# Graph attention and a quantised linear layer on one core: sums per 32 nodes on four column strips, last stage issued among the gathers

## The reference, cut to what matters

```
h   = layernorm(x);  xp = (h @ W).reshape(N, 4, 256)
e   = leaky_relu(a_src[src] + a_dst[dst])            # edges and one loop per node
ee  = exp(e - max over the edges of dst)
out[dst] = sum(ee * xp[src]) / sum(ee)               # per head
x   = x + relu(out + bias)
x   = x + fp6_blocks(layernorm(x)) @ fp6_blocks(weight).T + ffn_bias
```

## Time and profile before

| | us |
|---|---|
| three runs | 1359.40, 1360.31, 1364.32 |
| median | 1360.31 |
| span of the profiled execution | 1363.2 |
| `normalise` (until its last DVE operation ends) | 0 to 129 |
| `project` (until POOL starts its first gather) | 129 to 466 |
| `aggregate` (until the last sum is added) | 466 to 1052 |
| `finish` | 1052 to 1363 |

### The profile page before, as it was taken

How to read it: one execution, slowest core, us unless ns; L and a number is a source line. 1 busy time by engine, 2 the same in 40 slices (tenths; PEclk the granted TensorE clock), 3 DMA queues, 4 the chain that set the end, 5 groups by cost and what they waited for, 6 DMA issues and landing times. The chain is left out here.

```text
span 1363.2 us, 29337 instructions
## 1 busy us (share of the span) xinstructions
PE 1276.4 (94%) x10053; PEld 895.9 (66%) x10053; DVE 1070.2 (79%) x2221; ACT 988.2 (72%) x2239; POOL 747.8 (55%) x677
## 2 busy tenths in 40 slices
PE   7898888999999789999999899999996799999997
PEld 5776444554445378888888788888886344455543
DVE  6998899889844478888888788888885977777771
ACT  3666888884456388998888899899995566666661
POOL 1000766661247377777777777777772344444441
PEclk9899999999999899999999999999999899999999
DMA  7785586543454689999999999999998577777743
GB/s 260 248 301 191 167 309 193 187 154 133 153 210 171 245 323 381 378 368 361 376 360 380 394 401 375 375 336 369 376 369 314 158 192 190 188 191 189 190 101 53
DMA packets 111554, 361.54 MB, mean 265 GB/s; under 512 B 22108, under 2 KB 22892, under 8 KB 111156
## 3 DMA queue, kind: packets, MB, share of 16 engines
q0 software_dynamic: 68192, 225.42, 47.8%
q1 hardware_dynamic: 39860, 133.38, 28.1%
q10 hardware_dynamic: 3360, 0.91, 0.2%
HBM read 297.76 MB, written 72.82 MB: 272 GB/s over the span
## 5 line engine op out<-in xcount | busy, mean ns | idle before, releaser
L1800 PE MATMUL sum_ps<-xg,wgt 128*128 128x256 f16 x4992 | 561.4, 273 | 18.5 <-DMA xg<-d_xp,tables 10.7
L1771 ACT ACTIVATE wgt<-hot,tables 128x128 f16<-128x128 f16 x1664 | 503.1, 388 | 73.4 <-DVE hot L1715 63.2
L1800 PEld LDWEIGHTS sum_ps<-xg,wgt 128*128 128x128 f16 x4992 | 472.5, 98 | 75.3 <-DMA xg<-d_xp,tables 11.8
L1696 POOL DMA_INDIRECT xg<-d_xp,tables x404 | 418.0, 1035 | 127.5 <-issue 119.0
L1569 PE MATMUL xp_ps<-acc 128*128 128x512 f16 x1152 | 263.1, 381 | 8.2 <-DVE acc L1122 5.6
L1755 DVE TENSOR_TENSOR acc<-sum_ps,acc 128x1024 f32 x220 | 268.9, 1222 | 1.1 <-issue 1.0
L2198 PE MATMUL fmm_ps<-xg,tables 128*128 128x512 f16 x1200 | 263.1, 379 | 1.4 <-DVE tables L2027 1.4
L2198 PEld LDWEIGHTS fmm_ps<-xg,tables 128*128 128x128 f16 x1200 | 117.4, 98 | 137.8 <-issue 1.9
L1569 PEld LDWEIGHTS xp_ps<-acc 128*128 128x128 f16 x1152 | 109.3, 98 | 129.3 <-issue 4.9
L1726 DVE TENSOR_TENSOR wgt<-hot,tables 128x512 f16<-128x512 f16 x416 | 157.6, 418 | 0.0
L1929 POOL TENSOR_TENSOR tables<-tables,finv 128x1024 f32<-128x1024 f32 x24 | 45.9, 1914 | 131.8 <-DVE finv L2015 131.8
(11 more groups left out here) (328 smaller groups left out, 1586.7 us busy)
## 6 DMA issues: line engine op xcount, KB each, us to landing
d_xnT<-acc SPq DMA_DIRECT2D x25, 512.0 KB, 3.6
own_row<-d_own SPq DMA_DIRECT2D x25, 512.0 KB, 5.6
wdT<-in_x_dram SPq DMA_DIRECT2D x24, 512.0 KB, 4.9
acc<-d_xnT SPq DMA_DIRECT2D x24, 512.0 KB, 5.2
d_xp<-acc SPq DMA_DIRECT2D x24, 512.0 KB, 3.0
d_own<-acc SPq DMA_DIRECT2D x24, 512.0 KB, 4.3
xr<-in_x_dram SPq DMA_DIRECT2D x24, 512.0 KB, 6.7
out_dram<-acc SPq DMA_DIRECT2D x24, 512.0 KB, 6.7
```

What stands on the lines that cost most here:

```text
L1696: nc.gpsimd.indirect_dma_start(out=xg[s][u][:, :, :].rearrange("p a n -> p (a n)"), out_offset=None, in_=d_xp, in_offset=bass.IndirectOffs ...
L1771: last = nc.scalar.activation(wgt[k % WB][:, u, h, :], hot[k % TURN][:, u, :], ACT.Copy, scale=col(numT[:, h, :], u, q))
L1800: last = nc.tensor.matmul(sum_ps[s][:, h * C:(h + 1) * C], w[:, u, a * HEADS + h, :], x[u][:, b, h * C:(h + 1) * C], start=(u == 0 and h % ...
```

## The change

The sums are taken per window of 32 nodes. 98 windows cut the 391 groups into 488 slots, each of one group and one window, with one gather each; rows of a group outside the window are left out of the transfer. The four heads of a slot are four products with 32 columns of weights, whose outputs are PSUM partitions 0 to 31, 32 to 63, 64 to 95 and 96 to 127, all in one bank of 258 columns (256 and two for the sums of the weights). So the one-hots are 32 wide, all weights of a slot are 256 columns, and DVE makes both halves of them; ACT makes none. DVE adds 258 columns for each slot, at an index that it reads before each.

```diff
+WIN = 32
+TILE_WINS = P // WIN
+WINS = -(-N // WIN)
+GROUPS = -(-E // P)
+SLOTS_ALL = GROUPS + WINS - 1
+KCOLS = 4 * P
+KT = SLOTS_ALL
+AW = C + 2
+READY = [(r + 1) * SLOTS_ALL // SORTED for r in range(SORTED)] + [SLOTS_ALL]
+TURN_AT, MULTIPLY_AT = 16, 18
+RING = 6
...
+            def slot(k):
+                j, s, p, u = PLACES[k][0], sum_ps[k % SB], k // PAIR, k % PAIR
+                if u == 0:
+                    pe.wait_ge(wgt_ready, p + 1)
+                pe.wait_ge(arrived[j], landed[k])
+                if k >= SB:
+                    pe.wait_ge(added, k - SB + 1)
+                for i, (a, b) in enumerate(((0, 0), (0, 1), (1, 0))):
+                    for h in range(HEADS):
+                        nc.tensor.matmul(s[h * WIN:(h + 1) * WIN, 0:C], wgt[p % WB][:, u, a * HEADS + h, :], xg[j][:, b, h * C:(h + 1) * C],
+                                         start=(i == 0), stop=(i == 2), skip_group_check=True)
+                for h in range(HEADS):
+                    last = nc.tensor.matmul(s[h * WIN:(h + 1) * WIN, C:AW], hot[k // HOTS % HB][:, k % HOTS, :], numT16[:, k, h:V:HEADS, 0],
+                                            start=False, stop=True, skip_group_check=True)
+                last.then_inc(slot_done, 1)
...
+            def add(k):
+
+                w = dve.value_load(tile_row[0:1, k:k + 1], min_val=0, max_val=WINS - 1)
+                dve.wait_ge(slot_done, k + 1)
+                if k >= 1:
+                    dve.wait_ge(added, k)
+                to = sums[:, bass.ds(w, 1), :].rearrange("p o n -> p (o n)")
+                nc.vector.tensor_tensor(out=to, in0=sum_ps[k % SB][:, 0:AW], in1=to, op=ALU.add).then_inc(added, 1)
```

```diff
+    CHUNK = 5
+    MIX_AT, X1_AT, ROOT_AT, SCALE_AT, RESCALE_AT, LOW_AT, FINAL_AT = 1, 9, 11, 13, 15, 18, 30
+    BEGIN = READY[0:LAST] + [READY[LAST] + X1_AT + 1]
...
+            for k in range(SLOTS_ALL):
...
+                add(k)
+                for turns, do in due:
+                    for r in turns.get(k + 1, ()):
+                        do(r)
...
+            for k in range(SLOTS_ALL + MULTIPLY_AT + len(every)):
+                if k < SLOTS_ALL:
+                    slot(k)
+                for r in turns.get(k + 1, ()):
+                    turned(r)
+                for r, first, behind in chunks.get(k + 1, ()):
+                    products(r, first, behind)
```

More of the change, by code:

```diff
@@ L38, with ring_of_slots @@
 EP = EC * P
[L40 to L60, removed]
+WIN = 32
[6 more added lines that the diff above has]
+AW = C + 2
+assert SLOTS_ALL <= KCOLS and SLOTS_ALL % 4 == 0
+SORTED = TILES - 1
+READY = [(r + 1) * SLOTS_ALL // SORTED for r in range(SORTED)] + [SLOTS_ALL]
+TURN_AT, MULTIPLY_AT = 16, 18
+RING = 6
+SPARE_TILES = range(1, 6)
+def ring_of_slots():
+    free_from = [(0, j) for j in range(RING)] + [(READY[j] + TURN_AT + 8, RING + n) for n, j in enumerate(SPARE_TILES)]
+    used, places = {}, []
+    for k in range(SLOTS_ALL):
+        j = min((used.get(b, -1), b) for since, b in free_from if since <= k)[1]
+        places.append((j, used.get(j)))
+        used[j] = k
+    return places
+PLACES = ring_of_slots()
+FRESH = [k for k, (_, before) in enumerate(PLACES) if before is None]
 HCOLS = 17
@@ L242, in program @@
         if upto >= 3:
[L243 to L255, removed]
+            gather_and_finish(nc, maker, locals())
 def normalise(nc, maker, g):
@@ new lines, in _ @@
+            own.link(nc.vector.tensor_reduce(out=order_f[:, 0:SORTED], in_=compared, axis=AX.X, op=ALU.add))
+            nc.vector.tensor_copy(order_i[:, 0:SORTED], order_f[:, 0:SORTED])
+            dve.wait_ge(made, 3)
+            for c in range(CH):
+                last = nc.vector.tensor_scalar(inside[:, c, :], real(upto_f), kcol[:, c:c + 1], None, ALU.is_gt)
+            own.link(last)
+            for c in range(CH):
+                last = nc.vector.scalar_tensor_tensor(out=inside[:, c, :], in0=real(before_f), scalar=kcol[:, c:c + 1],
+                                                      in1=inside[:, c, :], op0=ALU.is_gt, op1=ALU.subtract)
@@ L1093, in _ @@
             for c in range(CH):
[L1094 to L1096 removed]
+                gather(nrow[c], halves(d_num), step_i[:, c:c + 1], rows_in)
             highest(range(5, TILES))
@@ L1610, in _ @@
                     last.then_inc(cinT_done, 1)
-                places = [(c, u, slice(u * P, (u + 1) * P), u * KCOLS + c * P) for c in range(CH) for u in range(SUB)]
                 if t == BUSY + 5:
@@ L1959, in _ @@
+            for k in range(SLOTS_ALL):
+                gather(k)
         @block.vector
@@ new lines, in final @@
+            def final(r):
+                dve.wait_ge(mm_done, OPENED + r + 1)
+                nc.vector.scalar_tensor_tensor(out=xr[r % 3], in0=mm_ps[:, :], scalar=out_scale[:, :], in1=xr[r % 3],
+                                               op0=ALU.mult, op1=ALU.add).then_inc(final_ready, 1)
+            steps = [(FINAL_AT, final), (LOW_AT, low), (RESCALE_AT, rescale), (SCALE_AT, scales), (ROOT_AT, root), (X1_AT, x1), (MIX_AT, mix)]
+            due = [(pieces(at), do) for at, do in steps]
@@ L2225, in _ @@
-            pe.wait_ge(ps_written, bias_set(LAST))
-            pe.wait_ge(low_ready, whole(LAST))
-            for half in range(2):
-                for c in range(KC):
-                    for a, b in ((0, 0), (0, 1), (1, 0)):
-                        last = product(LAST, c, a, b, half, c == KC - 1 and a == 1)
-                last.then_inc(mm_done, 1)
+            spin = numT16.rearrange("p k v b -> p (k v b)")
+            for half in range(2):
+                last = nc.tensor.matmul(mm_ps[:, half * 512:(half + 1) * 512], iota16[:, :], spin[:, 0:512], start=True, stop=True)
```

993 lines of the change are left out of this document (407 added, 586 removed).

## The result

The changed kernel takes 1542.8 us (median of 4 runs, 1541.0 to 1543.6), the one before 1359.9 beside it: a ratio of 1.1335, 95% interval 1.1316 to 1.1353. The forecast was 1495, in a range of 1310 to 1590, with 0.74 for slower. The profiled execution has a span of 1539.2 us, 41 us more than the 1498 of the sum. Among the executions of the last four experiments and of the kernel before beside them, two single ones took over 3300 us in a slow state; the times given leave them out.

What follows compares the result with a forecast made beforehand. PE was taken as full in the gathers and last stage, POOL full too. Start 481, plus 46 to slot 28, 22 tiles by 40.0 = 880, and 91 uncovered gave 1498, so 1495 us by median; range 1310 to 1590.

Steps and rivals of the forecast that it cites:

- End of the first stage: DVE's chain before the gathers: about 60 small operations replace some 30, net +14.5 us; POOL's first gather moves 466 to 481.
- the 46 us before slot 28: From POOL's first gather to the first tile's DVE-bound part: ten gathers, 6.1 us to land, 18 gathers by 1.33 us.
- A slot on PE: PE's products for one slot: 0.43 us if the four strips run beside one another, 1.39 if not.
- Strips one after another: Rival, chance 0.06: strips don't run side by side; 1.39 us a slot on PE, 49.6 us a tile, 1706 in all.
- A slot on DVE: Addition, weights and one-hots 0.67 us, plus a register load taken at 1.0: 1.15 us with the wait for one-hots.
- the first stretch: Slots 8 to 15 of a tile: DVE is the bound, PE has little to do; 16.7 us.
- loads hidden: Rival, chance 0.22: register load costs 0.4 us or less, DVE slot 0.67; 33.5 to 37.1 us a tile, 1352 to 1431.
- Stretch 2: Slots 16 to 18 of a tile: transposes, high and low part, with PE's products waiting for the low part; 4.5 us.
- Stretch 3: Ten pieces of products among nine slots, set by PE: 14.3 us, plus 1.9 for changes and 1.7 for clock, 17.9.
- Hand-overs: Added to a tile's three stretches for passing work between engines: 0.9 us, making 40.0 us a tile.
- The tail: What nothing covers at the end: the rest of tile 22, then tiles 23 and 24, 91 us.
- One bound: Rival, chance 0.16: stretches slide over one another, only the busiest engine counts; a tile takes 27 us, 1221 in all.

Runs made afterwards that it cites:

- the last four experiments: On a third chip, changed kernel with: twenty idle products before the transposes, 1510.1 us; early low part and late products, 1478.2; that with fixed windows, 1383.2, or packed loads, 1435.0.

## Why the prediction was right, and where its sizes were off

The mechanism is the one forecast: a tile is made of stretches that DVE and PE set in turn, 40.94 us of them against 40.0. The parts were off both ways, and some of the agreement is their cancelling.

*End of the first stage.* Forecast 14.5 us longer, POOL's first gather at 481. DVE's chain ends at 145.8 instead of 129.3, 16.5 longer, and the gather starts so:

```profile
480.75 1.09 POOL L1810 DMA_INDIRECT xg<-d_xp,first_idx  x1 [18.42 <-POOLq L894]
482.15 7.62 POOL L1810 DMA_INDIRECT xg<-d_xp,first_idx  x1 [0.30 <-issue]
```

The second gather holds POOL for 7.62 us, of which the sum had nothing; the addition of slot 28 comes at 532.1, not 527. The cause of that one was not tried. (The parts given for the 46 us before slot 28 add up to 43 or 44, so 2 us of the forecast had no source.)

*A slot on PE.* 0.43 forecast, 0.36 alone and 0.45 between products (0.44 and a gap to them of 0.1 as taken). "Strips one after another", 1.39 us, falls.

*A slot on DVE.* Here a size failed, the load at 1.0 us, from one row at a first use: between two additions the load adds 0.20 us and its address 0.11. The slot that the sum made of it was nearly right all the same, 1.15 against 1.04 measured, and that was luck: it let half of its dear load be covered (0.48 on a slot of 0.67), and the runs have a cheap one that nothing covers (0.32 on a slot of 0.72). Averaged over all slots of a tile, many of which wait for PE anyway, load and address cost 0.19 to 0.20 (3.85 and 4.16 us over 20.3). DVE's work of the tile's steps was right: 9.29 us from that tile's rows against 9.1. So the first stretch came out right, 15.34 us from the addition of x to the transposes. It holds 6 additions in half of the tiles and 7 in the others, and 16.7 less one and a half slots of the sum is 15.0. DVE is busy for 12.6 of it and idle for 2.8, of which 1.2 is "issue", as behind the moments:

```profile
818.99 0.43 DVE L1853 TENSOR_TENSOR acc<-sum_ps,acc 128x258 f32 x1 [1.02 <-issue]
```

The Trainium skill (Runtime: NRT & Kernel Launch, Instruction fetch mechanics) gives about 200 ns for each register, for loads from HBM. Here the loads come from SBUF; one between two additions adds 0.20 us, which agrees, but four in a row leave 2.61 us, 0.65 each, which does not. That a load of 200 ns would hide under the addition was wrong in either case. So the rival "loads hidden" failed at its own term: its condition (0.4 us or less) held, but its slot of 0.67 us was 1.04, and even with fixed places and nothing to hide it is 0.72. Its stretch 2 (4.1 for 5.60) and hand-overs were too short as well.

*Stretch 2.* 4.5 forecast, 5.60 measured (4.33 + 1.27). The difference is the clock: 1.97 for the transposes instead of 1.04, as the twenty products directly ahead showed by 4.33 falling to 3.21. Of a tile's terms this is the one that was off most.

*Stretch 3.* 17.9 forecast, 17.04 measured, by the terms of the sum: nine times 1.63 and a last piece are 15.5, which some tiles reach, and the mean is 1.5 above it, for the clock (1.7 taken): in the tile shown, the first five products, the slot behind them and the next five take 1.5 us more than the later ones. The gap at a change between strips and full products is 0.1 us (1.63 less 0.36 and 1.08, halved). The Trainium skill (TensorEngine Tiling (Array Packing), Key Properties) says that such a change drains the engine. A gap is there; the whole pipeline of 0.17 us that the prediction tried with it, 1.3 us more a tile, did not come.

*Hand-overs.* 0.9 forecast, 2.95 measured. But the 2.95 holds one to two slots that the sum counts in its first stretch, so the two are read together: 17.6 forecast, 18.29 measured. Behind the last product PE does its slots in 0.36 us, but DVE needs 0.82 or more for each addition and the addition of x also waits for ACT's moving (8.27 us for sixteen pieces). These two are +0.7 us a tile, stretch 2 +1.1 and stretch 3 −0.9; together +0.94, 20.7 us over 22 tiles.

*The tail.* 91 forecast, 106 measured. PE works there in part at the lower level too: the last 48 products, with a granted clock of 0.78, take

```profile
1513.27 13.43 PE L2047 MATMUL fmm_ps<-wdT,xqT 128*128 128x512 f16 x48 [4.87 <-ACT fmm_ps L1985]
```

13.43 us against the 10.4 of the sum. So 5 + 20.7 + 15.5 are the 41 us between 1498 and 1539.

*The rivals.* "One bound" asked that only the busiest engine count. DVE is busy 26.2 us of 40.94 and idle 14.7, of which 9.2 are put down to PE and 3.7 to "issue" or the addition before. Without loads and addresses, and with the low part early, a tile took 33.92, never 27. Its place, PE's wait for the low part, was real but was one of three: moving it later together with the transposes did nothing. The point from which the change gains was put at 33.9 us a tile; the run at 33.92 took 1383.2, because head and tail are 20 us longer than in the sum, so the point is near 32.9, which is 33.92 less (1383.2 − 1360) / 22.

*What stays open.* Where DVE's remaining 6 us a tile of waiting for PE would go with the high and low part on other engines was not tried, nor what the clock's whole fall costs, nor why 0.09 us stays between two additions with a fixed place, nor why PE and DVE have more "issue" and "remote" on the slower chips.

## What to carry to other kernels

Work laid under other work is hidden only where both have slack at the same time: with every step at a fixed place in each engine's order, a tile costs the sum of its stretches, each at the pace of its own busiest engine, plus the hand-overs. Add up the stretches, not the busy times, and look at the places where the first engine's lead is used up. Making the work of one engine smaller (PE from 95% busy to 62%) went with a lower clock (0.98 to 0.74), and the transposes behind the idle stretch took 1.97 us for 1.04. A register load of 0.20 us did not hide under the 0.43 us of the operation before it: take the price of a slot from the distance of two operations with a load between them, and not from the load alone.

## What was not expected of the hardware

- Two additions of 258 columns on DVE, 0.43 us each, start 0.52 us apart with fixed places, 0.63 with a place from a register whose value is there already, and 0.83 with its load too; four loads in a row leave 2.61 us.
- Three kinds of idle work for the clock: 35 products a tile that end over 7 us ahead of the transposes do nothing for them (1.97 us), 20 directly ahead restore them (1.04), and 3 us of waiting behind them leave the next products at the low level again (2.23 for 1.25).
- The same two kernels took 1.137 times as long (1546 for 1360, the one before) and 1.090 times as long (1682 for 1543, the changed one) on another chip, so that the same change has a ratio of 1.086 there and 1.134 on the first.
